# A pre-norm transformer layer on eight cores: shorter normalisation statistics, earlier background normalisations, and one more wait in the feed-forward groups

## The reference

```python
def _layernorm(x, axis=-1, eps=1e-5):
    m = jnp.mean(x, axis=axis, keepdims=True)
    v = jnp.var(x, axis=axis, keepdims=True)
    return (x - m) / jnp.sqrt(v + eps)

def attn(x, Wq, bq, Wk, bk, Wv, bv, Wo, bo):
    q, k, v = x @ Wq + bq, x @ Wk + bk, x @ Wv + bv   # split into heads, k and v repeated 4 times
    scores = einsum('bhqd,bhkd->bhqk', q, k) / sqrt(64)
    return einsum('bhqk,bhkd->bhqd', softmax(scores), v) @ Wo + bo

def ffn(h, gate_w, gate_scale, up_w, up_scale, down_w, down_scale):
    Wg, Wu, Wd = ((w - 128.0) * s[:, None] for each of the three)
    return (silu(h @ Wg.T) * (h @ Wu.T)) @ Wd.T

x = x + attn(_layernorm(x), ...)
x = x + ffn(_layernorm(x), ...)
```

## Time and profile before

| | |
|---|---|
| time before, two runs | 2667.41 and 2946.86 us, median 2807.13 |
| profiled execution | 2675.45 us |
| span of its slowest core (core 6) | 2673.9 us |
| spans of the eight cores | 2584.6 to 2673.9 us |
| TensorE busy | 2254.5 us, 84% |
| VectorE, ScalarE, GpSimd busy | 28%, 26%, 8% |
| TensorE in the chain that ended last | 74% (DMA 13%, VectorE 8%) |
| first transposes, projections | 0 to 379 us |
| attention | 380 to about 1000 us |
| output projection, second normalisation | to 1177 us |
| feed-forward | 1177 to 2674 us |

### The profile page before, as it was taken

One profiled execution on the slowest core, in us unless ns is written; L12 is line 12 of the kernel. 1 busy time (PEld: TensorE's weight loads), 2 busy tenths in 40 slices (PEclk: granted clock), 3 DMA queues, 4 the chain that ended last, 5 costly groups with the idle time before them and its releaser, 6 DMA issues.

```text
span 2673.9 us, 27825 instructions; the slowest of 8 cores (2584.6 to 2673.9 us)
## 1 busy us (share of the span) xinstructions
PE 2254.5 (84%) x10624; PEld 931.1 (35%) x10624; DVE 752.3 (28%) x913; ACT 683.1 (26%) x738; POOL 222.9 (8%) x233
## 2 busy tenths in 40 slices
PE   0687898888888858759979989989979789899897
PEld 0333432222222223334434434434434334344343
DVE  4434412222222213440410500502403303205018
ACT  2101038878887820121001011011010010010110
POOL 1020100000000000101011011011110110110100
PEclk9989989989888879869989989989989999899999
DMA  9396710000000063379379198296485674772943
GB/s 200 80 133 93 69 24 13 17 17 13 17 17 13 17 111 114 59 99 78 33 95 78 18 112 77 30 100 60 71 71 48 87 63 40 95 72 23 115 43 126
DMA packets 366112, 176.76 MB, mean 66 GB/s; under 512 B 342912, under 2 KB 347136, under 8 KB 361632
## 3 DMA queue, kind: packets, MB, share of 16 engines
q0 software_dynamic: 345680, 130.04, 46.4%
q1 hardware_dynamic: 20304, 44.95, 4.9%
HBM read 296.33 MB, written 8.65 MB: 114 GB/s over the span
## 4 chain that ended last, share of the span: by engine, by line
PE 74%; DMA 13%; DVE 8%; issue 3%; ACT 1%; DVEq 0%; SPq 0%; ACTq 0%; POOLq 0%
PE PS_C L207 21%; PE PS_A L207 20%; PE PS_B L207 19%; PE PS_D L207 10%; DMA arena<-uwt 7%; DVE arena L248 4%; DMA arena<-wq 2%; DMA arena<-xt 2%; DVE st L248 2%; DVE rrow L248 2%; PE PS_C L203 1%; DVE dscr L248 1%; PE PS_B L203 1%; PE PS_A L203 1%; DMA arena<-scr_r 1%
## 5 line engine op out<-in xcount | busy, mean ns | idle before, releaser
L207 PE MATMUL PS_A<-arena 128*128 128x512 bf16 (+1 forms) x2763 | 686.4, 394 | 155.8 <-DMA arena<-uwt 100.2
L207 PE MATMUL PS_C<-arena 128*128 128x512 bf16 (+1 forms) x2284 | 655.6, 400 | 107.3 <-DVE rrow L248 81.1
L207 PE MATMUL PS_B<-arena 128*128 128x512 bf16 (+1 forms) x2519 | 606.9, 384 | 2.8 <-ACT arena L235 1.7
L207 PEld LDWEIGHTS PS_A<-arena 128*128 128x128 bf16 (+1 forms) x2763 | 274.6, 100 | 568.3 <-issue 284.0
L207 PEld LDWEIGHTS PS_B<-arena 128*128 128x128 bf16 (+1 forms) x2519 | 246.4, 98 | 362.7 <-issue 88.6
L248 DVE TENSOR_TENSOR arena<-arena 128x1024 bf16<-128x1024 bf16 (+2 forms) x112 | 85.6, 764 | 954.3 <-ACT arena L235 952.6
L207 PE MATMUL PS_D<-arena 128*128 128x512 bf16 (+1 forms) x1258 | 328.0, 385 | 1.4 <-ACT arena L235 1.4
L235 ACT ACTIVATE arena<-PS_A,gs2b 128x1024 bf16<-128x1024 f32 x64 | 71.2, 1113 | 901.5 <-PE PS_A L203 901.5
L207 PEld LDWEIGHTS PS_C<-arena 128*128 128x128 bf16 (+1 forms) x2284 | 174.8, 104 | 357.3 <-issue 247.8
L235 ACT ACTIVATE arena<-PS_A 128x1024 bf16<-128x1024 f32 x171 | 185.4, 1084 | 97.4 <-PE PS_A L203 97.4
L235 ACT ACTIVATE arena<-PS_B 128x1024 bf16<-128x1024 f32 x171 | 185.5, 1085 | 33.3 <-PE PS_B L203 33.3
(11 more groups left out here) (53 smaller groups left out, 913.2 us busy)
## 6 DMA issues: line engine op xcount, KB each, us to landing
arena<-gwt POOLq DMA_DIRECT2D x64, 512.0 KB, 9.3
arena<-uwt POOLq DMA_DIRECT2D x64, 512.0 KB, 9.2
arena<-dwt POOLq DMA_DIRECT2D x64, 512.0 KB, 17.4
arena<-xt SPq DMA_DIRECT2D x24, 1024.0 KB, 8.1
arena<-wq POOLq DMA_DIRECT2D x32, 512.0 KB, 12.8
arena<-scr_r SPq DMA_DIRECT2D x64, 128.0 KB
out<-arena SPq DMA_DIRECT2D x8, 1024.0 KB, 3.8
arena<-wo POOLq DMA_DIRECT2D x1, 4096.0 KB, 30.7
```

What stands on the lines that cost most here:

```text
L207: e.matmul(o, ll, rr, start=a, stop=b, tile_position=t))
```

## The change

In `emit_ln` the four one-column operations become three, in another order: the squared sum (which no longer waits for ScalarE), the variance times 2048 by one fused operation, and the mean, which ScalarE's Ln does not wait for. The Ln's bias becomes 2048 times eps, and the Exp gets a bias of half the logarithm of 2048 from a second column of `epsb`, so that the factor is undone. In `qkv_block` a background normalisation is issued after Q column 3 too, not only after column 7, so that none is left after the last column. In the feed-forward part TensorE waits, before the first gate matmul of groups 1 to 7, for the last add of the group before.

```diff
-        epsb = sbuf("epsb", [P, 1], F32)
+        epsb = sbuf("epsb", [P, 2], F32)
...
-        v_op("memset", epsb[:], EPS)
+        v_op("memset", epsb[:, 0:1], D * EPS)
+        v_op("memset", epsb[:, 1:2], 0.5 * float(np.log(D)))
...
             a_sq = C['act']
+            v_op("tensor_mul", st[:, 4:5], st[:, 0:1], st[:, 0:1],
+                 inc=True, chain=True)
             v_wait(ACT, a_sq)
+            dve_v = v_op("scalar_tensor_tensor", st[:, 5:6], st[:, 4:5],
+                         -1.0 / D, st[:, 1:2], ALU.mult, ALU.add,
+                         inc=True, chain=True)
             v_op("tensor_scalar_mul", st[:, 2:3], st[:, 0:1], 1.0 / D,
                  inc=True, chain=True)
-            v_op("tensor_scalar_mul", st[:, 3:4], st[:, 1:2], 1.0 / D,
-                 inc=True, chain=True)
-            v_op("tensor_mul", st[:, 4:5], st[:, 2:3], st[:, 2:3],
-                 inc=True, chain=True)
-            dve_v = v_op("tensor_sub", st[:, 5:6], st[:, 3:4], st[:, 4:5],
-                         inc=True, chain=True)
             s_wait(DVE, dve_v)
             s_wait(DVE, war_st_dve)
             s_act(st[:, 6:7], st[:, 5:6], AF.Ln, bias=epsb[:, 0:1], inc=True)
-            a_r = s_act(st[:, 6:7], st[:, 6:7], AF.Exp, scale=-0.5, inc=True,
-                        chain=True)
+            a_r = s_act(st[:, 6:7], st[:, 6:7], AF.Exp, scale=-0.5,
+                        bias=epsb[:, 1:2], inc=True, chain=True)
...
-                    if miq == 7:
+                    if miq in (3, 7):
                         bg_step()
...
                 t_wait(ACT, act_silu.get(ic - 1, 0))
+                if sl == 0 and grp > 0:
+                    t_wait(DVE, dve_devac[(grp - 1, 7, 1)])
                 for hc in range(16):
```

## The result

| | before | after |
|---|---|---|
| median of all runs | 2685.4 us (15 runs) | 2647.66 us (17 runs) |
| profiled execution | 2675.45 us | 2647.66 us |
| span of its slowest core | 2673.9 us (core 6) | 2646.1 us (core 3) |
| ratio after/before | | 0.9897, 95% interval 0.9863 to 0.9931 |

In some executions the cores of one half of the chip are granted a lower clock (0.83 against 0.94 in after's execution of 2876 us), and the ratio leaves these out on both sides. It stands for a gain of 28 us (18 to 37). The forecast was 12 us (2663.4 us, range 2642 to 2696). So the time lies in the range, the sign is right, and the gain is more than twice the one forecast.

The account below looks back on a forecast made before the run. TensorE, busy 84% of the span, was taken to bound the kernel, so edits pay only at its stalls. Terms 3.4 + 2.2 + 11.4 - 5.0 - 0 = 12.0 us took 2675.45 to 2663.4 us, range 2642 to 2696.

Parts of the forecast that it names:

- up to the first K: At the start, shorter statistics on five tiles of the load chain save 0.43 us each: 2.2 us gained.
- second normalisation: VectorE carries the chain there; eight tiles save 0.43 us each: 3.4 us gained.
- two block boundaries: Blocks 0 and 1: no normalisation left ahead of the first transposed tile's copies, 5.7 us gained at each, 11.4 in all.
- Q columns of block 0: Moved x loads compete with Q weight loads on full DMA engines: 5.0 us lost, bounds 0 and 6.5.
- the new wait: Feed-forward groups 1 to 7: gate of slice 0 starts 3.4 us late, hidden by the shorter slice-2 wait; cost 0.
- the 6.1 us bounded: Feed-forward: 3.4 us delay plus at most 2.7 us of clock fall, under the shortest slice-2 wait of 7.42 us.
- the seven waits would shrink by 24 us: Sign in the profile after: feed-forward waits for up weights fall from 100.2 to about 75 us, group period unchanged.
- The statistics: Each of 24 normalised tiles: two small operations less save 0.52 us, Exp's bias column costs 0.09, net 0.43 us.
- Elsewhere it lies beside matmuls: Outside the start and the second normalisation, the shorter statistics were taken as hidden beside matmuls and counted for nothing.
- third rival: More is gained: added load only fills gaps, TensorE keeps its clock over the boundaries, about 1 us each; 2656 us, chance 0.15.
- The paid wait: Rival: the feed-forward wait is not hidden and costs 24 to 43 us, giving 2687 to 2706 us; chance 0.13.
- the Q stage eating the gain: Rival: the earlier loads of x tiles 12 and 13 cost 6.5 us each, 8.0 us more lost, 2671 us; chance 0.2.

Follow-up runs that it names:

- p3: Only the new wait before the gate matmuls of groups 1 to 7, added to the kernel before; ratio 0.9992 (0.9968 to 1.0016).
- n1: The kernel before without the down-weight loads of groups 1 to 7, which use group 0's weights (wrong result); ratio 0.9628 of before.
- n2: The new wait added to n1, so groups 1 to 7 load no down weights; ratio 0.9752 of before.
- p4: The whole change without the new wait: shorter statistics and moved background normalisations; ratio 0.9899 (0.9872 to 0.9926) of before.
- a1: The whole change again, the same program, on the chip of two spread-load kernels; ratio 0.988 (0.9843 to 0.9917) of before.
- the three `d` kernels: Whole change with down loads spread: two at a time 1.0226, one per slice 0.994, one per slice without the new wait 0.9828 of before.
- x1: The whole change with the loads of x tiles 12 and 13 held until block 0's Q columns are done; ratio 0.9944 of before.
- b1: Whole change without the new wait, one down load per slice, x tiles 12 and 13 held; fastest 2597.8 us, 0.983 between fastest runs.
- p2: Only the background normalisations moved (after Q columns 3 and 7), against the kernel before; ratio 0.9943 (0.9913 to 0.9972).
- p1: Only the shorter statistics (three one-column operations, Exp with a bias column), against the kernel before; ratio 0.9958 (0.9932 to 0.9984).
- d4: The whole change without the new wait, with one down-weight load at group start and one behind each of slices 0 to 6; ratio 0.9828 of before.

## Why the prediction was right, and where it was too small

The terms, against what the stages show. For the boundaries and the Q columns the last column compares the mean of before, `p3`, `n1` and `n2`, which have neither edit, with that of `p4`, after, `a1` and the three `d` kernels, which have both (`x1` and `b1` hold loads back and are left out); elsewhere the mean of all kernels without the new statistics with that of all with them but `b1`.

| term | forecast | from the traces |
|---|---|---|
| up to the first K | -2.2 | 91.5 to 87.9: -3.6 |
| second normalisation | -3.4 | 205.0 to 201.1: -3.9 |
| two block boundaries (the second with block 1's Q columns) | -11.4 | 14.2 to 6.9 and 81.1 to 73.6: -14.8 |
| Q columns of block 0 | +5.0 | 73.6 to 76.5: +2.9 |
| attention | 0 | 591.0 to 588.5: -2.5 |
| the new wait | 0 | whole runs: -2 (-9 to +4) |
| sum | -12.0 | -22; whole runs -28 (-18 to -37) |

**The new wait at 0: right, and for the reason given.** It delays the gate of slice 0 by 2.9 us and, by the clock, 1.5 to 1.7 more, together less than the 6.1 us bounded; the waits at slice 2 shrink by nearly as much (26 us of 31 in all), since the slice-2 weights are set by the backlog. `p3` shows no difference, the period from group to group doesn't grow by the 3 us that would have shown the forecast wrong, and `n2` against `n1`, without the backlog, shows the 33 us. The delay was 0.5 us shorter than forecast, since TensorE went on 0.14 us after the add and not the 0.47 of the earlier trace rows. I forecast that the seven waits would shrink by 24 us, from 100.2 to about 75. Between the two profiles they shrank by more, but before's profile has the longest of them of all kernels with the burst of eight, and over all cores of the kernels with and without the wait the difference is 26 us. This cover is that of the slower core of each pair: the faster ones of after have 5.6 to 14.3 us of such waits left in all seven groups together.

**The statistics: right per tile, perhaps short in the places where they count.** 0.43 us per tile is what the trace has, and the Exp did take 294 ns. That gap of 91 ns belongs to the bias operand and not to the function, as the Trainium skill ("ScalarE: Activation LUTs", What ACT_TABLE_LOAD costs) has it. What did not hold everywhere is the sentence "Elsewhere it lies beside matmuls". In the Q columns a background normalisation ends in a wait of TensorE for VectorE, 2.11 us in the earlier trace rows; with the shorter statistics it is 1.68. Over all cores with complete traces, before and `p2` have 14 such waits of 2.0 us or more at columns 6 and 10, and behind 7 of them the column ran slowly (up to 5.08 us for fifteen matmuls instead of 3.40). `p3`, `n1` and `n2`, with the old statistics too, have 16 more, 8 of them slow. In `p1`, `p4` and after there are 22 waits of 1.67 to 1.68 us at these columns, and none was followed by a slow column (a single one of 2.15 us was). One of each, block 1's column 10 in `p2` and block 0's column 10 in `p1`:

```profile
279.47 5.08 PE L207 MATMUL PS_A<-arena 128*128 128x512 bf16 x15 [2.11 <-DVE arena L248]
```
```profile
164.66 3.40 PE L207 MATMUL PS_A<-arena 128*128 128x512 bf16 x15 [1.68 <-DVE arena L248]
```

So half a microsecond less of waiting can be worth 2.1 us where the clock would have fallen. How much of the gain of `p1` came this way isn't shown: what it adds up to in the Q columns, about 1 us, lies within the scatter of single executions.

**The boundaries: the mechanism right, the size short by 3.4 us.** I priced them by the time that VectorE was held, 5.7 us each. The stages give 7.3 and 7.5. Of this `p2` alone has 6.5 and 6.8, and the statistics alone have 0.8 and 1.6. The wait itself shrank from 6.77 to 1.08 us, which is the 5.7. The rest goes with the clock: from the second transposed tile to the first K matmul it is 6.63 us in before, where seven transposes take 0.90 us or more, and 4.80 in after, where they take 0.55, so 1.8 us. The first K matmuls, in before and in after:

```profile
214.26 3.97 PE L207 MATMUL PS_B<-arena 128*128 128x512 bf16 x15 [0.36 <-DVE arena L248]
```
```profile
207.82 3.40 PE L207 MATMUL PS_B<-arena 128*128 128x512 bf16 x15 [0.36 <-DVE arena L248]
```

`p2` has only a part of this, as said above. This was in the text as a part of the third rival, at about 1 us each, and should have been in the sum, since the slow transposes stood in the earlier trace rows. It is the term that was mis-sized most. The statistics' share by themselves is the 0.43 us of the tile that stood there and something more, which no run took apart.

**The contention: right in kind, 5.0 us was too much.** The moved loads cost 2.9 us net in block 0 (2.0 in `p2` against the four kernels with neither edit, 4.0 in those with both against `p1`), and by `x1_hold` an x load costs 3.3 us there. The two stretches I took it from compare rates at full DMA engines; TensorE has columns in between at which it doesn't wait, and a part of the delay may go there, which was not tested. The Trainium skill ("DMA: Bandwidth & Descriptors", Issuing engines are not separate DMA queues) has it that the loads of both queues share the engines, and `x1_hold` agrees.

**Of the rivals,** the third ("more is gained", 2656) is nearest to what came in: a part of the contention gone, and the clock kept over the boundaries. But 2647.7 lies 8 us below it too. The paid wait is excluded by `p3`; the Q stage eating the gain is excluded by `p2`.

**The range held with some luck.** Its low side was said to be the lowest case less some 8 us of scatter, and 2656 - 8 is 2648, where 2642 was written. The measured 2647.7 lies in the range by what was added to that working.

**What stays open.** The attention stage is 2.5 us shorter in the kernels with the new statistics, although nothing in it was edited. Its Exps take 1077 to 1087 ns in the mean over all these kernels; no run told the cause. And the sum of the stages, 22 us, is 6 us short of the whole runs, inside their interval. It leaves out the feed-forward stage, which is 7.6 us shorter in after than in before. The same stage is 7.5 and 18.8 us shorter in `p1` and `p2`, which edit nothing there, and 0.8 longer in `p3`. These are single executions, and no run told whether more than scatter stands behind it.

## What to carry to other kernels

A wait costs nothing as long as a later wait on the same engine ends at a time set by something else; look for what sets that later time, and say what the wait costs once it is gone, since the next improvement (here the spread loads) will uncover it. When a stall of TensorE is priced, its matmuls behind the stall belong to the price, and an edit that shortens a stall by half a microsecond can save several times as much when it keeps the clock up. Loads that are moved out of a stall into a stage with full DMA engines pay there with a part of what the move gains. And a mean over cores is only comparable when it takes the same kind of cores on both sides.

## What the runs showed of the hardware that was not expected

In most profiles the two cores of a pair are not alike, and which is slower changes. In before's profile they took 2650.6 and 2584.6 us (cores 0 and 1), in after's 2575.1 and 2630.6. They are not unlike in all: in `d4` three of the four pairs lie within 2 us. Most of the difference arises where the loads queue: the slower cores wait 49 to 57 us for up weights in after, the faster ones 6 to 14. Without the down loads of seven groups all eight cores lie between 2534.2 and 2562.6 us. The time of the kernel is that of the slower core of a pair, so a wait read on the slowest core of one profile has to be set beside that of the slower cores of the other.

Spreading a burst of loads made the kernel 60 us slower than before with two loads per slice, and with one it was 16 us faster than before with the new wait and 46 without it. The down loads of seven groups cost 99 us in all (`n1`, which leaves them out); the best of the three orders, `d4`, was 19 us faster than `p4` by their ratios, with overlapping intervals.
